# A fused two-layer kernel: column sums of the second weight bank taken from raw pieces on GpSimd, and the first tiles' matmuls and mixings in another order

## The reference

```python
att = softmax(gelu(gelu(cond @ W0 + b0) @ W1 + b1) @ W2 + b2)        # 64 x 8
agg_w = einsum('bk,koi->boi', att, weight); agg_b = att @ bias_k      # per sample 64 x 64, 64
c = einsum('boi,bih->boh', agg_w, x) + agg_b[:, :, None]              # mixing of the channels
h = relu(layernorm(c @ gw1.T + gb1) * gamma + beta)
gates = h @ gw2.T + gb2                                               # top 2 of 8 experts
out = c @ weight.T + lora(c, w(gates)) / 16
x = x + out
```

## Time and profile before

| what | value |
|---|---|
| median of 3 runs | 1265.34 us (1264.83 to 1265.67) |
| time of the profiled execution | 1265.09 us |
| its span in the trace | 1263.3 us |
| PE busy | 1257.2 us (100%), 6967 matmuls |
| PEld busy | 1165.1 us (92%) |
| DVE busy | 842.7 us (67%), 2171 instructions |
| ACT busy | 307.3 us (24%) |
| POOL busy | 235.2 us (19%), 170 instructions |
| granted TensorE clock, mean | 1.00 of full |

### The profile page before, as it was taken

One profiled execution on the slowest core, in us unless ns is written; L12 is line 12 of the kernel. 1 busy time (PEld: TensorE's weight loads), 2 busy tenths in 40 slices (PEclk: granted clock), 3 DMA queues, 4 the chain that ended last, 5 costly groups with the idle time before them and its releaser, 6 DMA issues.

```text
span 1263.3 us, 21216 instructions
## 1 busy us (share of the span) xinstructions
PE 1257.2 (100%) x6967; PEld 1165.1 (92%) x6967; DVE 842.7 (67%) x2171; ACT 307.3 (24%) x654; POOL 235.2 (19%) x170
## 2 busy tenths in 40 slices
PE   9999999999999999999999999999999999999998
PEld 8999999999999999888889889888888888988987
DVE  6877866667667667756765765675676576576563
ACT  6323332222223234211121121121121112112110
POOL 1244522232323222011001001001100100100100
PEclk9999999999999999999999999999999999999999
DMA  8355433333334267434223323322423322332310
GB/s 278 129 145 167 146 110 116 128 122 120 114 109 132 91 217 223 123 90 123 71 80 114 88 71 106 106 71 89 122 71 88 116 78 71 113 99 71 98 43 34
DMA packets 84889, 141.55 MB, mean 112 GB/s; under 512 B 6769, under 2 KB 53361, under 8 KB 84849
## 3 DMA queue, kind: packets, MB, share of 16 engines
q1 hardware_dynamic: 84848, 141.04, 36.7%
HBM read 88.57 MB, written 52.45 MB: 112 GB/s over the span
## 4 chain that ended last, share of the span: by engine, by line
PE 97%; DVE 1%; DMA 1%; ACT 0%; SPq 0%; issue 0%
PE ps L1345 30%; PE ps L1347 29%; PE ps L1346 29%; PE ps L1514 5%; PE ps L1516 2%; DMA xo<-in_xt 1%; DVE weights L960 1%; PE ps L1503 0%; PE ps L1480 0%; PE ps L1610 0%; DVE mixs L970 0%; PE ps L1505 0%; DVE mixw L969 0%; SPq L432 0%; ACT L800 0%
## 5 line engine op out<-in xcount | busy, mean ns | idle before, releaser
L1345 PE MATMUL ps<-weights,lhs_h 128*128 128x512 f32 (+3 forms) x1408 | 498.5, 354 | 0.0
L1347 PE MATMUL ps<-weights,lhs_l 128*128 128x512 f32 (+3 forms) x1408 | 489.1, 347 | 0.0
L1346 PE MATMUL ps<-weights,lhs_h 128*128 128x512 f32 (+3 forms) x1408 | 489.0, 347 | 0.0
L1345 PEld LDWEIGHTS ps<-weights,lhs_h 128*128 128x128 f32 x1408 | 264.5, 188 | 23.9 <-issue 0.6
L1347 PEld LDWEIGHTS ps<-weights,lhs_l 128*128 128x128 f32 x1408 | 264.5, 188 | 21.3
L1346 PEld LDWEIGHTS ps<-weights,lhs_h 128*128 128x128 f32 x1408 | 265.2, 188 | 19.8
L715 POOL TENSOR_TENSOR xo<-row,wsum 128x512 f32<-128x512 f32 x60 | 76.8, 1306 | 647.3 <-DMA out_x<-xo 647.3
L1345 PE MATMUL ps<-weights 128*128 128x384 f32 (+1 forms) x376 | 128.8, 343 | 0.0
L1346 PE MATMUL ps<-weights 128*128 128x384 f32 (+1 forms) x376 | 128.1, 341 | 0.0
L1347 PE MATMUL ps<-weights 128*128 128x384 f32 (+1 forms) x376 | 127.9, 340 | 0.0
L1231 DVE TENSOR_TENSOR whole<-ps,whole 64x256 f32<-64x256 f32 x240 | 101.2, 422 | 7.7
(11 more groups left out here) (201 smaller groups left out, 1622.7 us busy)
## 6 DMA issues: line engine op xcount, KB each, us to landing
row<-spill SPq DMA_DIRECT2D x30, 576.0 KB, 4.2
z<-x_round SPq DMA_DIRECT2D x64, 256.0 KB, 5.1
out_x<-xo SPq DMA_DIRECT2D x31, 512.0 KB, 2.7
xo<-in_xt SPq DMA_DIRECT2D x30, 512.0 KB, 3.5
x_round<-row SPq DMA_DIRECT2D x60, 256.0 KB, 2.1
row<-in_xr SPq DMA_DIRECT2D x31, 400.0 KB, 3.2
spill<-row SPq DMA_DIRECT2D x31, 400.0 KB, 3.8
staging<-in_w SPq DMA_DIRECT2D x9, 832.0 KB, 6.1
```

The source lines that it names most:

```text
L1345: pe.matmul(out_ap, lhs[0], rhs[0], start=first, stop=False, skip_group_check=True)
L1346: pe.matmul(out_ap, lhs[0], rhs[1], start=False, stop=False, skip_group_check=True)
L1347: return pe.matmul(out_ap, lhs[1], rhs[0], start=False, stop=last, skip_group_check=True)
```

## The change

Bank 1's column sums are no longer made from the split weights by 16 matmuls. GpSimd adds up the raw pieces of chunks 8 and 9 as they lie in `staging`: three adds of 128 x 832 and one of 128 x 416 (`added_rows`). ScalarE takes the high part of that total, GpSimd the low part (`total_high`, `total_low`), and TensorE multiplies ones by the two (`added_sums`, 2 matmuls of 416 columns). The low part of chunk 11 moves from VectorE to GpSimd (`by_pool`), as does the product of line 969 for tile 3 (`mix_product(3)`). The DMA of chunk 11 also waits for the first of the adds, which reads the buffer it overwrites. Scratch rows of the conditioning move from `whole` to `mixw`. TensorE's order at the start changes: bank 1's product of tile 0 stands before its first mixing, and the column sums of bank 2 come after the second mixing. VectorE takes `y_low(1, 0)` and `y_low(2, 0)` earlier, ScalarE makes the square root's table load and `bias12_of(0)` before `root(0)`.

```diff
@@ -121,6 +121,9 @@
+        pairs = whole[:, :, :].rearrange("p j t -> p (j t)")[:, 0:2 * WIDE0].rearrange("p (k n) -> p k n", k=2)
+        total = pairs[:, 0, :]
+        total_hl = [lora_b[:, s * WIDE0:(s + 1) * WIDE0] for s in range(2)]
...
@@ -375,7 +379,7 @@
-        by_pool = (N_LB0, N_CONV, N_LB1, N1, N1 + 4)
+        by_pool = (11, N_LB0, N_CONV, N_LB1, N1, N1 + 4)
...
@@ -471,6 +475,7 @@
             load_xr0(0, 0)
+            sp.wait_ge(added, 1)
             chunk(11)
...
@@ -672,10 +677,31 @@
+            def added_rows():
+
+                first, second = staged(8), staged(9)
+                pool.wait_ge(stage_in[where[8]], 16)
+                pool.tensor_tensor(pairs[:, :, :], first[:, 0:2, :], first[:, 2:4, :], ALU.add).then_inc(added, 1)
+                pool.wait_ge(stage_in[where[9]], 16)
+                for c in range(2):
+                    pool.wait_ge(added, c + 1)
+                    pool.tensor_tensor(pairs[:, :, :], pairs[:, :, :], second[:, 2 * c:2 * c + 2, :],
+                                       ALU.add).then_inc(added, 1)
+                pool.wait_ge(added, 3)
+                pool.tensor_tensor(total, total, pairs[:, 1, :], ALU.add).then_inc(added, 1)
+
+            def total_low():
+                pool.wait_ge(added_hi, 1)
+                pool.tensor_tensor(total_hl[1], total, f32(total_hl[0]), ALU.subtract).then_inc(added_lo, 1)
+
+            added_rows()
+            row_init0(0, 0, 0)
+            split_lo(11)
+            row_init0(1, 1, 0)
+            total_low()
             pool.wait_ge(consts_in, 16)
             pool.wait_ge(attc_ready, 1)
-            row_init0(0, 0, 0)
-            row_init0(1, 1, 0)
+            mix_product(3)
             row_init12(0, 0, 0)
             row_init0(2, 0, 1)
...
@@ -815,15 +845,17 @@
             split_hi(11)
+            total_high()
             bias0_of(1)
+            y_high(0, 1)
+            x_high(3, 3, 1)
+            act.activation(sc[:, 5:6], eps[:, :], ACT.Sqrt).then_inc(tables, 1)
+            bias0_of(2)
+            column_sums(2)
             column_sums(1)
-            x_high(3, 3, 1)
-            bias0_of(2)
-            y_high(0, 1)
-            root(0)
-            column_sums(2)
             act.wait_ge(wsum_ready, 3)
             bias12_of(0)
+            root(0)
...
@@ -1060,18 +1093,17 @@
             split_lo(8)
+            y_low(1, 0)
             split_lo(9)
...
             mix_matrix(0, 0)
-            y_low(1, 0)
             split_lo(10)
+            y_low(2, 0)
             mix_matrix(1, 1)
             evict(0, 0, 0)
-            split_lo(11)
-            y_low(2, 0)
             mix_matrix(2, 2)
...
@@ -1387,6 +1419,15 @@
+            def added_sums(k):
+
+                n = COLS0[k]
+                pe.wait_ge(added_lo, 1)
+                for s in range(2):
+                    mm = pe.matmul(ps[:, BM0[k], 0:n], ones[:, :], total_hl[s], start=s == 0, stop=s == 1,
+                                   skip_group_check=True)
+                mm.then_inc(wsum_done, 1)
...
@@ -1458,17 +1499,22 @@
-            column_sums(1)
+            main(0, 0, 1)
             pe.wait_ge(zeroed, 4)
             mix(0, 0, 0)
+            main(0, 0, 2, 0, 4)
+            mix(1, 1, 0)
+            column_sums(2)
+            added_sums(1)
 
             def phase_a(t, b, it):
-                main(t, b, 1)
                 if at(t, 0):
-                    mix(1, 1, 0)
-                    column_sums(2)
-                mix(t + 2, (b + 2) % XB, 0)
-                main(t, b, 2)
+                    main(0, 0, 2, 4, 8)
+                    mix(2, 2, 0)
+                else:
+                    main(t, b, 1)
+                    mix(t + 2, (b + 2) % XB, 0)
+                    main(t, b, 2)
                 mix(t, b, 1)
```

More of the change, by code:

```diff
@@ L231, in program @@
         ctxo = cbuf[0:B, 954:1018]
-        wbuf = whole[:, :, :].rearrange("p j t -> p (j t)")
+        wbuf = mixf
         att_m = wbuf[0:B, 0:TILES * KATT].rearrange("b (t k) -> b t k", k=KATT)
@@ L249, in program @@
         wsum_done, wsum_ready = sem("wsum_done"), sem("wsum_ready")
+        added, added_hi, added_lo = sem("added"), sem("added_hi"), sem("added_lo")
         biased0, biased12 = sem("biased0"), sem("biased12")
@@ L770, in column_sums @@
             def column_sums(k):
-                act.wait_ge(wsum_done, k + 1)
+                act.wait_ge(wsum_done, (1, 3, 2)[k])
                 act.activation(wsum[:, START0[k]:START0[k + 1]], ps[:, BM0[k], 0:COLS0[k]],
@@ L777, in root, with total_high @@
                 act.activation(sc[:, 0:1], mv[:, 1:2], ACT.Sqrt, bias=eps[:, 0:1]).then_inc(std_ready, 1)
+            def total_high():
+                act.wait_ge(added, 4)
+                act.activation(total_hl[0], total, ACT.Copy).then_inc(added_hi, 1)
             act.wait_ge(zeroed, 2)
@@ L962, in mix_matrix @@
             def mix_matrix(t, b):
-                if later(t, XB):
-                    dve.wait_ge(mix_terms, t - AHEAD)
-                    dve.wait_ge(mix_done[2], t - AHEAD)
+                if later(t, 3):
+                    dve.wait_ge(mix_terms, t - 2)
+                    if later(t, XB):
+                        dve.wait_ge(mix_done[2], t - AHEAD)
                 else:
@@ L1086, in links_before @@
                 caught_up = isinstance(t, int) and t > CATCH_UP
-                return A_BASE + t * A_LINKS + (1 if later(t, 1) else 0) + (ROUTE_LINKS if caught_up else 0)
+                return A_BASE + t * A_LINKS + (ROUTE_LINKS if caught_up else 0)
             def phase_a(t, b, it):
@@ L1100, in phase_a @@
                 if at(t, 0):
+                    y_low(0, 2)
                     mix_matrix(3, 3)
-                    y_low(0, 2)
                     evict(0, 0, 1)
@@ L1128, in phase_a @@
                         x_low(t + XB, b)
-                assert at(t, CATCH_UP) or links["n"] == A_LINKS + at(t, 0), links["n"]
+                assert at(t, CATCH_UP) or links["n"] == A_LINKS, links["n"]
             periods(dve, phase_a)
@@ L1434, in mix @@
                 if at(t, 0):
-                    pe.wait_ge(wsum_ready, k + 1)
+                    pe.wait_ge(wsum_ready, 3 if k else 1)
                 elif not is_end(t, k):
```

## The result

The changed kernel takes **1273.86 us** (median of 4, 1273.53 to 1274.23), the kernel before 1265.2 beside it (4 runs, 1264.83 to 1265.67). The ratio is 1.0068, with a 95% interval of 1.0056 to 1.0080: slower by 8.7 us. The profiled execution took 1273.59 us, 8.50 more than that of before.

A forecast was written before the change was run, and what follows sets the result against it. TensorE bounds the kernel, VectorE second in the early stretch. `main(3)` 5.8 us later (-2.87 + 5.6 + 2.05 + 1.2 gives 6.0), restarts about 0.08 each and 0.3 make +6.3: 1271.4, 1271.6 us as median; range 1265.0 to 1276.5.

The forecast's parts named there:

- What bounds the kernel: TensorE bounds the whole, VectorE is second between 20 and 30 us; removed matmuls and a wait give 2.87 us at most.
- Prices on GpSimd: Estimated times of GpSimd's new adds, subtraction, chunk 11's low part and product, 12.9 us in sum.
- Meetings: VectorE and GpSimd instructions that meet wait for the other's end, then need their own time less some 0.13 us.
- Step 1: At the conditioning, VectorE's product (18.30) just precedes GpSimd's first add, which runs 18.6 to 20.6 us.
- the first add beats the conditioning's product: At 18.30 us, named among reasons for the forecast range's upper end, with a delay of 7.5 us.
- Steps 2 and 3: Adds alternate with VectorE's low parts, then tile 0's casts and subtractions with GpSimd's long instructions; second subtraction at 34.95 us.
- Steps 4 to 6: TensorE waits 5.6 us at the first mixing, 2.05 for chunk 10's low part, 1.2 before the second mixing.
- Step 7: After the second mixing, 6.84 us of matmuls from 40.9; `main(3)` starts at 47.7 instead of 41.92, +5.8 us.
- small term for what comes behind `main(3)`: TensorE's waits in tiles 1 and 2, since VectorE comes out later against it than before: 0.3 us.
- The clock rival: TensorE's clock falls to its lower level in the 5.6 us gap: 1272.6 to 1275 us; chance 0.22.
- The gain: GpSimd's work really runs beside VectorE's, tile 0's matrix is ready before 29.3, whole 2.87 gained: 1262.5 us; chance 0.14.
- VectorE wins the ties: Tile 0's casts, subtractions and chunk 10's low part precede GpSimd's longest pass; waits 1.5 and 1.3: 1265.3 us; chance 0.09.

The follow-up runs named there:

- experiment 9: Changed kernel with adds started behind the conditioning's product, chunk 11's low part on VectorE, bank 1's sums by TensorE's 16 matmuls again: 1271.57 us (1270.78 without those matmuls).
- experiment 1: Changed kernel, but GpSimd starts its adds only once VectorE has written the conditioning's product: 1274.9 us.
- experiment 2: Changed kernel with 11 filler matmuls before the conditioning's step and 14 before the second mixing: ratio 1.0079, one execution of 7151.32 us left out.
- experiment 3: Changed kernel with chunk 11's low part back on VectorE, behind the first eviction: 1270.71 us.
- 8: Changed kernel without the adds, bank 1's sums by TensorE's matmuls, plus 20 filler matmuls before the second mixing: 1269.45 us.
- 4: Changed kernel without the adds, bank 1's sums by TensorE's matmuls behind bank 2's; chunk 11's low part and product 3 stay on GpSimd: 1271.51 us.
- experiment 10: Changed kernel with GpSimd's adds replaced by memsets, started behind the conditioning's product, and chunk 11's low part on VectorE: 1267.39 us.
- experiment 6: Kernel before with one edit, chunk 11's low part made by GpSimd instead of VectorE: 1267.63 us.

## Why the prediction was right, and where it was not

The verdict (slower) and the range held; the forecast, 1271.6, was 2.3 us short. The mechanism, GpSimd's instructions standing in VectorE's way and VectorE holding up TensorE, is what the runs show. That the number came so near is in part luck: in the changed kernel the meetings fell on other instructions than in the prediction, and of its three waits (5.6, 2.05 and 1.2) only the last came, with 2.33. By its steps:

- **What bounds the kernel.** Right, and it is the core of the case: TensorE is the bound over the whole, VectorE in this stretch. Where the prediction gave 2.87 us for the removed matmuls and subtracted them in full, experiment 9 got 0.8 of them, not told from nothing. The prediction's sum stayed right there, since it took the waits as they followed from VectorE's times, so that matmuls removed came back as waits.
- **Prices on GpSimd.** 832 elements took 1.96 (estimate 1.98), the product 1.27 (1.30), the subtraction 1.06 (1.08), the pass of 1536 elements 3.42 in experiment 1 (3.50). All but the product, which had a row of its own, were estimated from the neighbours' rows.
- **Meetings.** Right, and shown: two low parts of 1.88 us beside memsets, and of 2.17 and 3.20 beside adds. The list of what meets GpSimd was too short, though: it had no operation like the one on 64 x 8 elements of the conditioning, which takes a single tensor from SBUF.
- **Step 1 failed.** "the product at 18.30 is ahead by a hair, so the first add runs 18.6 to 20.6". The prediction's own margin was 0.1 us, and it let the chunk's arrival stand as before. The chunk was there at 17.82, 0.18 us before the 64 x 8 operation that stands in front of the product, and that operation was caught; in the kernel before it came 0.36 us after that operation's start (18.40 against 18.04), and in experiments 2 and 3, where the product itself was caught, 0.15 to 0.19 after. So the order of the two is decided by some tenths of a microsecond in the arrival of a transfer. The case stood in the prediction as a bound ("the first add beats the conditioning's product") without its consequence: TensorE waits 1.87 us, and its clock falls. It decided the course of the kernel more than its time: experiment 1, without it, takes 1.0 us longer.
- **Steps 2 and 3**, the second subtraction behind chunk 11's pass: not in the changed kernel. The slow TensorE delayed `y_high(2, 0)` on ScalarE (to 30.93), which delayed the high part of chunk 11 and so the pass, to 32.88 instead of 30.3. By then tile 0's matrix was done (31.6), and the pass met tile 1's product instead (3.55 for 0.69). In experiment 1, which has the assumed order, it happened as written (4.32 for the pair).
- **Steps 4 to 6**, waits of 5.6, 2.05 and 1.2: none, none and 2.33 in the changed kernel; 5.47, 1.69 and none in experiment 1. In the changed kernel TensorE came to the first mixing at 35.41, itself late by the slow clock, and found it ready.
- **Step 7**, `main(3)` 5.8 us late, 0.24 for restarts and 0.3 behind it: 7.12 and 1.38. So of the 2.2 us that the sum lacks (8.50 against 6.3), 1.1 are lost by `main(3)` and 1.1 behind it. The small term for what comes behind `main(3)` was sized too low, in experiment 1 as well (2.6 us).
- **The clock rival** (0.22) had the right behaviour, but it thought of the gap of 5.6 us, and here 1.87 did it. Its sign (matmuls of 384 columns 0.35 us apart) is there, at 0.32. What it cost in the changed kernel stays open: 4.41 + 1.56 us of slowness are in the table, but experiment 2 removed the first and gained nothing, while the meetings moved. Where VectorE is not late behind it (8 against 4), it is worth 2.06 us.
- **The gain** (0.14) and **VectorE wins the ties** (0.09): neither. For the gain it would not have been enough that GpSimd's work be beside VectorE's: experiment 10, where it nearly is, takes 1267.4 us and not 1262.5.

## What to carry to other kernels

Work moved from VectorE to GpSimd is not off VectorE when both read SBUF: 1.75 us moved cost 3.3 us of standing for a neighbour of 0.69. Look at what VectorE has to do in the time in which the moved instruction runs; the longer the moved one, the more it costs, and short instructions lose the most for their size (two subtractions of 64 x 64 took 4.32 us for 0.47). And matmuls removed from a stretch in which TensorE is about to wait for VectorE are worth little (0.8 of 2.67 us, not told from nothing).

## What was not expected of the hardware

- An instruction of 64 x 8 elements with one input is held up by a whole GpSimd add (1.79 us for 0.22), and a copy of 128 x 8 likewise (1.39 for 0.16).
- The granted clock fell after a wait of 1.87 us in the changed kernel, and not in the profiled execution of experiment 3 after one of 1.78 at the same place, nor in that of experiment 6 after one of 1.86 before the second mixing. The ten executions of experiment 6 differ: the five that took 1267.86 to 1268.90 us have a mean clock of 0.998 or 0.999, and four of the five that took 1266.80 to 1267.39 have 1.000. What decides within one kernel stays open.
